# Layer 0 of a four-layer graph network: softmax sums inverted in two groups per half and spread through DRAM by DMA, chunks weighed in pairs

## The reference, cut to what matters

```python
h = max(layernorm(x), 0)
q, k, v = (h @ W.T + b, in 4 heads of 32 features)      # one W and b for each
scores = clip(q @ k.T / sqrt(32), -10, 10)              # [4, 1024 rows n, 8 chunks j of 128 columns c]
scores = where(adj == 0, -10, scores)
attn = softmax(scores, axis=-1)                         # within each chunk of 128 columns, not over the row
ctx = einsum('bhnjc,bhjcd->bhnd', attn, v_chunks)       # the 8 chunks are added
out = layernorm(ctx @ Wo.T + bo + h) * gamma + beta
x = x + out
```

## Time and profile before

| | |
|---|---|
| median of 3 runs | 2159.24 us (2152.0 to 2163.05) |
| the profiled execution | 2157.34 us, its span 2155.5 us |
| mean granted clock of TensorE | 0.902 of full speed |
| busy, of the span | TensorE 81%, VectorE 74%, ScalarE 62%, GpSimd 5% |
| layer 0 | from the start to about 789 us |
| copies of q and k (L288) | 128 each of 128 KB, 2.3 us from issue to landing |
| spreading products (L412) | 256, 68.7 us busy, TensorE idle 48.1 us before them |
| weighings (L725), into `weighed` alone | 96 of 128, 65.8 us busy, 96.0 us idle before them |

### The profile page before, as it was taken

One profiled execution on the slowest core, in us unless ns is written; L12 is line 12 of the kernel. 1 busy time (PEld: TensorE's weight loads), 2 busy tenths in 40 slices (PEclk: granted clock), 3 DMA queues, 4 the chain that ended last, 5 costly groups with the idle time before them and its releaser, 6 DMA issues. The chain is left out here.

```text
span 2155.5 us, 37200 instructions
## 1 busy us (share of the span) xinstructions
PE 1736.7 (81%) x13876; PEld 1102.1 (51%) x13876; DVE 1595.2 (74%) x2790; ACT 1346.2 (62%) x1767; POOL 111.6 (5%) x130
## 2 busy tenths in 40 slices
PE   2888888888888827699899977797877776999997
PEld 1344343443344325577677755675656553555554
DVE  2676767677767746678888889988988965767674
ACT  2665645555455517577677778988889834545553
POOL 0000000101000010000000000000000000000000
PEclk9999989999899957899999988998988988999999
DMA  6413031130311021111111112221112202000000
GB/s 191 98 40 79 1 79 40 41 79 1 79 40 40 1 82 55 35 40 50 41 40 41 50 51 70 70 70 61 61 60 70 79 26 79 11 10 20 10 10 20
DMA packets 50270, 108.92 MB, mean 51 GB/s; under 512 B 7633, under 2 KB 26450, under 8 KB 50098
## 3 DMA queue, kind: packets, MB, share of 16 engines
q1 hardware_dynamic: 50098, 106.54, 17.1%
HBM read 68.37 MB, written 4.59 MB: 34 GB/s over the span
## 5 line engine op out<-in xcount | busy, mean ns | idle before, releaser
L1052 ACT ACTIVATE g<-s_all,steep_d 128x1024 fp8e4<-128x1024 f32 x608 | 642.3, 1135 | 42.1 <-DMA s_all<-s_rows 26.4
L993 PE MATMUL acc<-parts,g 128*128 128x102 bf16 (+1 forms) x6144 | 418.0, 229 | 28.5 <-DVE sums L1143 19.3
L993 PEld LDWEIGHTS acc<-parts,g 128*128 128x128 fp8e4 x6144 | 401.6, 99 | 61.6 <-issue 43.8
L975 PE MATMUL post<-parts,edge 128*128 128x396 bf16 (+1 forms) x1024 | 232.9, 383 | 83.7 <-DVE base L1151 83.7
L558 ACT ACTIVATE e<-s_ps 128x1024 f32<-128x1024 f32 x256 | 248.9, 1022 | 37.0 <-PE s_ps L390 26.6
L1136 DVE TENSOR_TENSOR g<-g,edge 128x1024 int32<-128x1024 int32 x192 | 227.7, 1218 | 34.6 <-ACT g L1052 34.6
L564 ACT ACTIVATE chunk<-ctx_ps 128x512 f32<-128x512 f32 x128 | 76.2, 596 | 243.1 <-PE ctx_ps L420 243.1
L386 PE MATMUL s_ps<-qs,ks 128*128 128x512 f32 x512 | 207.4, 517 | 12.4 <-issue 7.5
L975 PEld LDWEIGHTS post<-parts,edge 128*128 128x128 fp8e4 x1024 | 102.2, 102 | 191.3 <-issue 106.6
L704 DVE SCALAR_TENSOR_TENSOR e<-e,bound 128x1024 f32<-128x1024 f32 x160 | 189.8, 1220 | 8.4 <-ACT e L558 8.4
L420 PE MATMUL ctx_ps<-e,v 128*32 128x512 f32 x1024 | 152.7, 668 | 48.8 <-DVE weighed L725 42.0
(11 more groups left out here) (157 smaller groups left out, 2208.8 us busy)
## 6 DMA issues: line engine op xcount, KB each, us to landing
s_all<-s_rows SPq DMA_DIRECT2D x96, 512.0 KB, 3.6
qs<-split SPq DMA_DIRECT2D x128, 128.0 KB, 2.3
ks<-split SPq DMA_DIRECT2D x128, 128.0 KB, 2.3
x<-in_x SPq DMA_DIRECT2D x8, 512.0 KB, 6.0
adj_in<-in_adj SPq DMA_DIRECT2D x8, 512.0 KB, 4.1
out_x<-x SPq DMA_DIRECT2D x8, 512.0 KB, 3.2
parts<-in_adj_t SPq DMA_DIRECT2D x6, 512.0 KB, 6.0
chunk<-in_adj_t SPq DMA_DIRECT2D x4, 512.0 KB, 6.5
```

Source lines behind the costliest of these rows:

```text
L975: ins = pe.matmul(self.post[:, it % 2, 0:H * 3 * W1].rearrange("p (h k c) -> p h k c", h=H, k=3), self.c.edge[:, jt, it * P:(it + 1) * P], ...
L993: ins = pe.matmul(self.acc[:, bank, o:o + self.NS], self.g[:, h % RING, jt, it * P:(it + 1) * P], self.upper[par][:, jt, h, :, :].rearrang ...
L1052: act.activation(self.g[:, h % RING, jt, :], self.s_all[:, h % 2, :], ACT.Relu, bias=self.steep_d[par][:, jt, h:h + 1], scale=STEEP, satur ...
```

## The change

Everything is in layer 0. The inverses no longer go through TensorE:

- `sums` collects four chunks in place of eight before the bank `sum_ps` is read (`GROUP = 4`; row `4q + j`). VectorE takes the reciprocal four times a graph (after the first clip of steps 4, 8, 12 and 0) and nothing else: the rounding and the rest go, `inv` is plain float32.
- SyncE stores each reciprocal (128 x 256) to DRAM, waits until it has landed, and loads it back spread over the 32 partitions of each head: for each pair of chunks four loads, one for each head, into one of two buffers (`inv_all`, one by the parity of the pair). A load waits until the pair that used the buffer before has been weighed.
- VectorE weighs two chunks in one instruction, [128, 2 chunks, 512], from SBUF alone. Pairs 0 to 3 of the first half are weighed in steps 7, 9, 11, 13, those of the second in step 15 and in steps 1, 4, 6 of the next stage. All but pair 0 are followed by an addition of the same size.
- `ctx_ps` holds value products only. `spread`, its constants and the 16 activations that made it are gone, as is SyncE's wait for them ahead of the loads of x for graphs 2 to 7.
- On SyncE the transfers of the inverses stand among q's and k's copies: those of steps 0, 4 and 8 ahead of q's copies, that of step 12 behind k's copies.

Core of the diff, in the file's order:

```diff
+    GROUP = T // 2
+    FIRST_HALF, SECOND_HALF = (7, 9, 11, 13), (15, 1, 4, 6)
...
-        def weighed_at(i):
-
-            return int(1 <= i <= 8), (i - 1) % T
+        def pair_at(i):
+
+            if i in FIRST_HALF:
+                return 0, FIRST_HALF.index(i)
+            return 1, SECOND_HALF.index(i)
...
+            def inverses(b, half, group):
+                m = 2 * b + half
+                n = 2 * m + group
+                wait_apart(c, sp, inverted, n + 1)
+                sp.dma_start(inv_dram[half, group].rearrange("h r n -> (h r) n"), inv[:, :]).then_inc(inv_stored, 16)
+                wait_apart(c, sp, inv_stored, 16 * n + 16)
+                for p in (2 * group, 2 * group + 1):
+                    wait_apart(c, sp, pair_weighed, 4 * m + p + 3)
+                    j = 2 * (p % 2)
+                    for h in range(H):
+                        rows = inv_dram[half, group, h, 0:2 * GROUP, :].rearrange("(q j) n -> q j n", q=2)[:, j:j + 2, :]
+                        sp.dma_start(inv_all[h * DH:(h + 1) * DH, p % 2, :, :],
+                                     rows.rearrange("q j n -> q (j n)").partition_broadcast(DH)).then_inc(
+                                         inv_loaded[p % 2], 16)
             def stage(b, par, first, more):
                 if first:
-                    sp.wait_ge(selected, 16)
                     for n in range(2, B):
                         load_x(n, x_loaded[2])
                     sp.wait_ge(const_steps, 6)
                     for k in range(3):
                         sp.dma_start(const3[k:k + 1, :], const_parts[:, k, :]).then_inc(const_stored, 16)
+                else:
+                    inverses(b - 1, 1, 1)
+                inverses(b, 0, 0)
+                inverses(b, 0, 1)
                 if more:
-                    prepare(b + 1, 1 - par)
-
-            walk(sp, prepare, stage)
+                    wait_apart(c, sp, s_ready, 32 * b + 64)
+                    stack_q(b + 1, 1 - par)
+                    stack_k(b + 1, 1 - par)
+                inverses(b, 1, 0)
+
+            def tail():
+                inverses(B - 1, 1, 1)
+
+            walk(sp, prepare, stage, tail)
...
             def sums(b, i):
                 half, jt = divmod(i, T)
                 pe.wait_ge(p_ready, 32 * b + 2 * i + 2)
-                if jt == 0:
-                    pe.wait_ge(sums_read, 2 * b + half + 1)
+                if jt % GROUP == 0 and not (isinstance(b, int) and b == 0 and i == 0):
+                    pe.wait_ge(inverted, 4 * b + i // GROUP)
                 for q in range(2):
                     for h in range(H):
-                        at = 16 - 8 * q - jt
+                        at = 16 - GROUP * q - jt % GROUP
                         ins = pe.matmul(sum_ps[h * DH:(h + 1) * DH, :], pick[:, at:at + DH],
                                         e[:, 2 * (i % 2) + h // 2, h % 2, q * QUARTER:(q + 1) * QUARTER],
-                                        start=(jt == 0 and q == 0), stop=(jt == T - 1 and q == 1),
+                                        start=(jt % GROUP == 0 and q == 0), stop=(jt % GROUP == GROUP - 1 and q == 1),
                                         tile_position=(0, h * DH))
                 ins.then_inc(summed, 1)
-            def spread_inverses(b, i):
-                half, j = weighed_at(i)
-                pe.wait_ge(inverted, 2 * b + half + (1 if i >= 9 else -1))
-                for q in range(2):
-                    ins = pe.matmul(ctx_ps[:, q * QUARTER:(q + 1) * QUARTER], spread[:, q, j, :], inv_sum[:, :],
-                                    start=True, stop=True)
-                ins.then_inc(inv_spread, 1)
-
             def values(b, par, i):
                 pe.wait_ge(chunk_copied, 16 * b + i + 1)
-                pe.wait_ge(chunk_weighed, 16 * b + i + 1)
...
-                    if first and i == 9:
-                        pe.wait_ge(selected, 16)
-                    if not (first and i < 9):
-                        pe.wait_ge(chunk_copied, 16 * b + i)
-                        spread_inverses(b, i)
                     if not (first and i == 0):
                         sums(before[0], before[2])
                         values(*before)
...
-                act.wait_ge(late_loaded, 128)
-                for x in range(16):
-                    act.activation(spread[:, x // 8, x % 8, :], same_head, ACT.Copy,
-                                   scale=row_is[:, x:x + 1]).then_inc(selected, 1)
...
             def copy_chunk(b, i):
                 act.wait_ge(pv_done, 16 * b + i + 3)
-                act.wait_ge(chunk_weighed, 16 * b + i + 1)
+                act.wait_ge(pair_weighed, 8 * b + i // 2 + 1)
...
-            def invert(b, half):
-                m = 2 * b + half
-                dve.wait_ge(summed, 8 * m + 8)
-                if not (isinstance(m, int) and m == 0):
-                    dve.wait_ge(ctx_ready, m)
-                dve.reciprocal(inv, sum_ps).then_inc(sums_read, 1)
-                dve.wait_ge(sums_read, m + 2)
-                dve.tensor_copy(inv_hi, inv).then_inc(inv_cut, 1)
-                wait_apart(c, dve, inv_cut, m + 1)
-                dve.scalar_tensor_tensor(out=inv_sum[:, :], in0=inv_hi.bitcast(F32), scalar=minus_low[:, 0:1],
-                                         in1=inv, op0=ALU.mult, op1=ALU.add).then_inc(inverted, 1)
+            def invert(b, half, group):
+                n = 4 * b + 2 * half + group
+                dve.wait_ge(summed, GROUP * n + GROUP)
+                if not (isinstance(n, int) and n == 0):
+                    dve.wait_ge(inv_stored, 16 * n)
+                dve.reciprocal(inv[:, :], sum_ps).then_inc(inverted, 1)
             def weigh(b, i):
-                half, j = weighed_at(i)
-                m = 2 * b + half - (0 if i >= 9 else 2)
-                dve.wait_ge(inv_spread, 8 * m + j + 1)
-                if j in (4, 6):
-                    dve.wait_ge(added, 2 * m + j // 2 - 1)
-                dve.tensor_tensor(ctx_sb[:, half, j, :] if j < 2 else weighed[:, j % 2, :], chunk[:, j, :], ctx_ps[:, :],
-                                  ALU.mult).then_inc(chunk_weighed, 1)
-                if j >= 3 and j % 2 == 1:
-                    dve.wait_ge(chunk_weighed, 8 * m + j + 9)
-                    acc = ctx_sb[:, half, :, :]
-                    ins = dve.tensor_tensor(acc, acc, weighed[:, :, :], ALU.add)
-                    ins.then_inc(added if j < 7 else ctx_ready, 1)
+                half, p = pair_at(i)
+                m = 2 * b + half - (0 if i >= 7 else 2)
+                dve.wait_ge(inv_loaded[p % 2], 64 * (2 * m + p // 2 + 1))
+                dve.wait_ge(chunk_copied, 8 * m + 2 * p + 3)
+                if p > 1:
+                    dve.wait_ge(added, 2 * m + p - 1)
+                acc = ctx_sb[:, half, :, :]
+                by_quarter = lambda t: t.rearrange("p j (q n) -> p q j n", q=2)
+                dve.tensor_tensor(by_quarter(weighed[:, :, :] if p else acc), by_quarter(chunk[:, 2 * p:2 * p + 2, :]),
+                                  inv_all[:, p % 2, :, :].rearrange("p q (j n) -> p q j n", j=2), ALU.mult).then_inc(pair_weighed, 1)
+                if p:
+                    dve.wait_ge(pair_weighed, 4 * m + p + 5)
+                    dve.tensor_tensor(acc, acc, weighed[:, :, :], ALU.add).then_inc(added if p < 3 else ctx_ready, 1)
...
-                    if not (first and i < 9):
+                    if first and i == 7:
+                        dve.wait_ge(const_stored, 48)
+                    if i in FIRST_HALF or i in SECOND_HALF and not (first and i < 7):
                         weigh(b, i)
                     clip(b, i, 0)
                     if i == 8:
-                        if first:
-                            dve.wait_ge(const_stored, 48)
-                        invert(b, 0)
+                        invert(b, 0, 1)
+                    elif i in (4, 12):
+                        invert(b, i // T, 0)
                     elif i == 0 and not first:
-                        invert(b - 1, 1)
+                        invert(b - 1, 1, 1)
...
-                for i in range(9):
-                    weigh(B, i)
-                    if i == 0:
-                        invert(B - 1, 1)
-                        update(B - 2, 1)
-                    elif i == 3:
-                        residual(B - 1, 1, 0, False)
-                    elif i == 6:
-                        update(B - 1, 0)
+                invert(B - 1, 1, 1)
+                update(B - 2, 1)
+                weigh(B, 1)
+                residual(B - 1, 1, 0, False)
+                weigh(B, 4)
+                weigh(B, 6)
+                update(B - 1, 0)
                 residual(B - 1, 1, 1, False)
                 update(B - 1, 1)
```

52 lines of the change are left out of this document (19 added, 33 removed).

## The result

The changed kernel took 2104.74 us (median of 4 runs, 2103.01 to 2112.04) against 2157.74 for the kernel before: a ratio of 0.9768 with a 95% interval of 0.9738 to 0.9799, about 53 us faster. The profiled execution took 2103.01 (span 2101.2). The prediction was 2113. The loss in part A, the start and the end came as it said; the gain of part B was put too small, and the list of steps behind it placed TensorE's waits in the wrong steps.

What follows compares the result with a forecast made beforehand. TensorE and VectorE take turns, neither full, and part A is tied to q's copies. Seven periods -26.6, start -4.3, last graph and end -13.4 sum to -44.3 us, giving 2113; range 2095 to 2135.

Steps and rivals of the forecast that it cites:

- part A: Layer 0, end of step 8's reciprocal to step 11's value products: 19.1 us before, predicted 0.9 longer per period.
- the start: Start of layer 0: without 16 activations building spreading matrices, the scores end the wait for the first exponential; -4.3 us.
- the end: Last graph, from last sums to last projection: 29.0 us of single-file spreadings and weighings become 15.6; -13.4.
- part B: Layer 0, step 11's value products to the next graph's step 8 reciprocal: 70.2 us before, 65.5 predicted, -4.7 per period.
- the list of steps: Part B, VectorE against TensorE step by step: VectorE's excess 10.3 us in steps 13, 0, 1, 2, 4, 5, 6.
- TensorE loses 6.2 in B: Part B: 24 spreading products go, and TensorE's busy time falls from 60.7 to 54.5 us.
- The same -4.7 for seven periods: Part B's -4.7 us counted alike in all seven periods; with part A's +0.9, -26.6.
- The page's rule: Store of inverses: one section estimates 2.3 us for 128 KB; the other would make A some 2 longer per period.
- Inverses after k's copies, at nothing: Step 12's inverses, behind k's copies, weighed in step 15: no cost beyond B's hand-overs, VectorE's wait there under 2 us.
- (1): Rival: SyncE's queue decides, between step 8's reciprocal and q's copies and before step 15; slower, 2174 us; chance 0.09.
- (2): Rival: VectorE's lumps eat part B's gain, leaving only start, end and A; 2146 us; chance 0.15.
- (3): Rival: TensorE keeps its clock and the list is loose, B 60.8 in all periods; 2080 us; chance 0.14.

Runs made afterwards that it cites:

- e11: Changed kernel with the weighing of steps 13 and 1 done three times over, 2.5 us more VectorE work in each: 2142.8 us, ratio to before 0.9948.
- e4: Changed kernel with all stores and loads of the inverses issued by GpSimd instead of SyncE: 2094.9 us, ratio to before 0.9712.
- e7: e1 with, in addition, the inverses of step 12 stored and loaded among k's copies: 2073.0 us, ratio to before 0.9636.
- e1: Changed kernel with the four loads of pair 3 issued behind q's copies instead of ahead of them: 2086.0 us, ratio to before 0.9670.
- e2: Changed kernel with step 8's inverses stored a second time, elsewhere, and awaited before pair 2's loads: 2113.2 us, ratio to before 0.9813.
- e12: Changed kernel with the weighing of steps 4 and 6 done three times over, 2.5 us more VectorE work in each: 2153.3 us, ratio to before 1.0001.
- e3: Changed kernel with two unused 128x256 products before each step's value products, putting TensorE's spreading work back without weighing: 2116.8 us, ratio to before 0.9816.
- e5: Changed kernel with q's 16 copies moving only half the columns, 64 KB each, from graph 2 on: 2097.4 us, ratio to before 0.9749.
- e9: e7 with the 8 copies of q's low part issued by GpSimd beside SyncE's 8 of the high part: 2067.8 us, ratio to before 0.9602.

## Why the prediction was right, and where it was off

*TensorE loses 6.2 in B, to 54.5.* 55.0 measured. Right.

*VectorE's list: an excess of 10.3 in seven steps, 0.7 for hand-overs.* This is the step that was off. TensorE's idle time in B is 8.5 on average (63.5 less 55.0), not 11.0, and in the period shown it stands in steps 15, 3, 4 and 6, not in 13, 0, 1, 2, 4, 5 and 6. The times of the list were right: VectorE needs 4.7 in step 13 (listed 4.75), 5.8 in step 0 (5.7), 4.6 in step 2 (4.65) and 5.3 in step 4 (5.45). What the list left out is VectorE's lead, the time by which its clips are done before TensorE comes to their sums. It charged every step by itself, as if both engines entered it together, while a step costs nothing until the lead is used up. The sums and clips of steps 12 and 13, of 0, and of 2, in order of time, then the clock between the sums of steps 15 and 0:

```profile
452.00 1.07 PE L432 MATMUL sum_ps<-e,pick 128*32 128x256 f32 x16
452.41 2.35 DVE L706 SCALAR_TENSOR_TENSOR e<-e,bound 128x1024 f32<-128x1024 f32 x2
454.99 1.07 PE L432 MATMUL sum_ps<-e,pick 128*32 128x256 f32 x16
472.00 1.16 DVE L706 SCALAR_TENSOR_TENSOR e<-e,bound 128x1024 f32<-128x1024 f32 x1
474.92 1.07 PE L432 MATMUL sum_ps<-e,pick 128*32 128x256 f32 x16
480.81 2.36 DVE L706 SCALAR_TENSOR_TENSOR e<-e,bound 128x1024 f32<-128x1024 f32 x2
483.23 1.07 PE L432 MATMUL sum_ps<-e,pick 128*32 128x256 f32 x16
...
468.23:474.92 6.69, 6.69 (x32) 2.30 (x33) 5.67 (x12) 1.48 (x2) 0.00 (x0) 0.56 0.06 21
```

The clips of step 12 end at 450.11, 1.9 before their sums; those of step 13 end at 454.76, 0.2 before theirs: the excess of 1.8 came out of the lead. The lead of step 0 is 1.8 (473.16 to 474.92), because TensorE at its lower clock took 6.7 from the sums of step 15 to those of step 0 where the list had 4.05; in step 2 it is down to 0.1. So the list's 1.7 + 0.8 + 1.7 of steps 0 to 2 left only 0.59, before the sums of step 3. Where no lead was left the list is near: 1.30 for 1.65 in step 4, 2.87 for 2.0 + 0.7 in steps 5 and 6. The sum also held TensorE's slow stretches twice, once in the 54.5 and once in an excess taken against steps at full clock; they are 1.6 behind part A's stop and 2.6 behind step 15 (an estimate: the 3.7 and 6.7 that these stretches took, less 2.1 and 4.05 for the same work at full clock). e11 bears this out: it adds 2.5 in step 13, where a lead of 0.1 to 1.2 was left (0.2 in this period), and the wait there is 2.25; the whole of it is paid because the excess before it had used the lead up. The list left out step 15, whose sums wait 3.98, 2.05 of it for late inverses. That the sum of B came out within 2 us is thus in part luck: some 5.5 of excess without a wait against 4.0 of wait without an entry.

*The same -4.7 for seven periods.* Measured -6.5. Six of them fell by 6.1, the last by 9.1 (68.2 to 59.1). Its second half, in graph 7, prepares no further graph, so VectorE has less to do in it; the prediction made no exception of it. Of the 12.8 us by which the sum of the B terms was off, 4.4 are this one period and 8.4 the other six.

*Part A, +0.9.* +1.2. Its pieces: store and wait 1.95 (I took 2.2), eight loads 3.6 (3.3), and as means of seven periods: start of q's copies 6.0 after the reciprocal (5.5), issue 10.5 (10.7), landing 2.5 after it (1.8), ScalarE's wait 8.5 (7). The landing time was taken from a stretch in which the DMA engines were 0.75 busy (453.7 to 464.5 before the change), and used in one where they are full (1.00 or more from 432 to 442 after it); this alone is 0.7 of A on average and 1.4 in graph 4.

*The page's rule.* The Trainium skill, "DMA: Bandwidth & Descriptors", section "Anatomy of one DMA", gave an estimate of 2.3 for the store of 128 KB; this case's store was followed by its loads after 1.95, and in e4, issued by GpSimd, it landed in 2.1 (median). The other section, "Latency and other measured facts", would have made it some 2 longer under load; no run here shows that case, since the DMA engines stood at 0.20 while the store was on its way (425.5 to 427.5).

*Inverses after k's copies, at nothing.* VectorE waits in step 15 in every period, 15.4 in all, 6.6 of it in the first graph. e7, which takes nearly all of it away, lowers B by 0.9 against e1. Off by about 6 over the seven periods. My sign of "under 2" failed in three of the seven (6.6, 2.3 and 2.05).

*The start, -4.3.* 3.5 at the first exponential and 4.5 at step 8. It is not the scores that end the wait, as I had it, but a table load that stands before the exponential (51.97).

*The last graph and the end, -13.4.* -13.4 measured, 16.0 from the last sums to the last projection against 15.6.

*The rivals.* (1) did not come, since the store and eight loads took 5.9 and not 11.8; but e1 and e2 show that its mechanism is real: 1.6 earlier gave 1.9, and 2.3 later cost 2.1. e4 shows its bound: 3.7 earlier gave nothing, since the data then held the copies. (2) fell: B is 6.5 shorter. e11 and e12 show that VectorE's lumps do decide B once its lead is used up. (3) did not come: the clock in B stayed as it was (0.92 before, 0.91 after), and TensorE's first products after the stop in A run at the lower level (1.93 for eight value products, 1.04 at the higher).

What stays open: how the gain of B divides between the spreading's busy time and the waits for the weighing; e3 couldn't keep them apart because the clock moved with it.

## What to carry to other kernels

When a step is moved onto a DMA queue, look at what is issued behind it and for whom, and order the transfers by who needs them first: half of the loads ahead of q's copies were needed two steps later, and moving them behind gave 19 us. A wait that two limits pin (issue count and bytes) doesn't move when one of them is lifted; try both together before calling either harmless. A list of steps needs the lead of one engine over the other carried from step to step, and each engine's time at the clock that it will have there; a step's excess costs only what the lead doesn't cover. It also needs the first and the last pass as rows of their own, and landing times from a stretch as loaded as the new one.

## What the runs showed of the hardware

- The issue of sixteen copies between partitions took SyncE 10.05 at 64 KB (e5) and 10.08 at 128 KB (changed kernel) in graph 4, 0.63 each, and 10.5 on average over seven periods in both. Loads of 128 KB that read DRAM went in 0.45 each.
- The same 128 KB copy landed in 2.3 (before), 3.2 (after), 6.4 (median of the sixteen in e4's part A), by what else was in flight. In the changed kernel 3.28 MB moved between 425 and 445, and the busy share of the DMA engines was 0.54 from 428 to 430, 0.75 to 432 and 1.00 or more from there to 442.
- In e9 GpSimd issued eight such copies in 4.45, 0.56 each, SyncE at the same time eight in 6.89, 0.86 each; alone SyncE took 0.63 (changed kernel).
- In e12 a stop of TensorE of 4.1 was followed by three groups at the lower clock (1.94, 1.94 and 2.05, against 1.07, 1.05 and 1.20). A stop of 2.87 in the changed kernel was followed by none (1.07 for the sums), but one of 2.83 in e12, three groups of normal length after the slow ones, again by groups of 1.94 and 1.85.
